# A window-attention kernel: 26 fewer pairs of always-met waits ahead of the causal attention, and each layer's weights requested in eight parts

## The reference: what is computed

```
x = layernorm(x + causal_attention(x))      # 16 heads of 8, rotary, full causal softmax
x = layernorm(x + window_layers(x))         # 6 layers, see below
x = layernorm(x + memory(x))                # circular convolution and a decayed sum over time
x = layernorm(x + routed_experts(x))        # 8 experts, top 2, limited capacity
```

```
x = attn_layer(shift_tokens(x), Wqkv[i], q_scale[i], k_scale[i], Wo[i]) + x
x = ffn_layer(shift_tokens(x), ln_g[i], ln_b[i], W1[i], b1[i], W2[i], b2[i]) + x
```

## Time and profile before

| | |
|---|---|
| median of three runs | 2211.4 us (2200.99, 2211.4, 2215.6) |
| profiled execution | 2203.34 us, its span 2201.5 us |
| mean granted TensorE clock | 0.939 of full speed |
| PE / DVE / ACT / POOL busy | 88% / 79% / 68% / 58% of the span |
| causal attention | from the start to about 412 us |
| window layers | about 415 to 2000 us |
| memory and experts | the rest |

### The profile page before, as it was taken

One profiled execution on the slowest core, in us unless ns is written; L12 is line 12 of the kernel. 1 busy time (PEld: TensorE's weight loads), 2 busy tenths in 40 slices (PEclk: granted clock), 3 DMA queues, 4 the chain that ended last, 5 costly groups with the idle time before them and its releaser, 6 DMA issues. The chain is left out here.

```text
span 2201.5 us, 68287 instructions
## 1 busy us (share of the span) xinstructions
PE 1941.5 (88%) x26493; PEld 1304.8 (59%) x26493; DVE 1738.5 (79%) x3617; ACT 1502.7 (68%) x2952; POOL 1267.1 (58%) x1132
## 2 busy tenths in 40 slices
PE   5788898589999999999999999999999999984283
PEld 2333333246777777777677776777677777762162
DVE  4666654578999999999899998999999999844623
ACT  2256556457888788878787877888788878854123
POOL 4500000278777877787677777777777787711053
PEclk8699989889999999999999999999999999996587
DMA  6312100201111121111211113111311111101612
GB/s 159 110 43 45 23 3 2 70 28 41 31 41 31 40 69 52 32 41 31 81 41 40 32 31 91 31 41 31 91 31 41 31 41 31 41 21 27 195 37 69
DMA packets 70612, 108.18 MB, mean 49 GB/s; under 512 B 20887, under 2 KB 47774, under 8 KB 68734
## 3 DMA queue, kind: packets, MB, share of 16 engines
q1 hardware_dynamic: 68262, 100.87, 16.0%
q0 software_dynamic: 1280, 2.62, 0.4%
q10 hardware_dynamic: 752, 0.33, 0.1%
HBM read 41.60 MB, written 12.26 MB: 24 GB/s over the span
## 5 line engine op out<-in xcount | busy, mean ns | idle before, releaser
L1730 POOL TENSOR_TENSOR qk<-rot_cos,rot_sin 128x512 f32<-128x512 f32 x256 | 324.2, 1274 | 95.9 <-DVE rot_sin L1476 95.3
L1740 POOL TENSOR_TENSOR qk<-qk,rnorm 128x512 f32<-128x512 f32 x256 | 263.1, 1044 | 139.4 <-DVE rnorm L1509 139.4
L1474 DVE TENSOR_TENSOR rot_cos<-pA,layer_tab 128x512 f32<-128x512 f32 x384 | 264.0, 688 | 55.7 <-ACT sq L1258 42.0
L437 ACT ACTIVATE probs_by_key<-pT 128x512 f32<-128x512 f32 (+3 forms) x384 | 177.3, 489 | 159.3 <-PE pT L320 124.5
L1486 DVE TENSOR_REDUCE sumsq<-sq 128x8 f32<-128x512 f32 x384 | 257.6, 672 | 30.5 <-ACT sq L1258 30.4
L502 DVE TENSOR_REDUCE minus_max<-pS 128x1 f32<-128x1024 f32 (+7 forms) x256 | 184.7, 754 | 117.7 <-PE pS L290 117.0
L1476 DVE TENSOR_TENSOR rot_sin<-pA,layer_tab 128x512 f32<-128x512 f32 x384 | 261.5, 681 | 0.0
L1258 ACT ACTIVATE sq<-pA 128x512 f32<-128x512 f32 x384 | 231.4, 602 | 29.3 <-PE pA L880 22.7
L1316 ACT ACTIVATE probsT<-pD 64x512 f32<-64x512 f32 x384 | 226.4, 590 | 6.7 <-PE pD L925 4.5
L880 PE MATMUL pA<-W_ahead,x_feature_major 128*128 128x512 f32 x384 | 202.6, 611 | 17.1 <-DVE rot_sin L1476 10.8
L941 PE MATMUL pD<-probsT,v 128*64 128x64 f32 x3072 | 196.4, 223 | 18.0 <-issue 16.6
(11 more groups left out here) (318 smaller groups left out, 4576.4 us busy)
## 6 DMA issues: line engine op xcount, KB each, us to landing
v_shifted<-v SPq DMA_DIRECT2D x96, 384.0 KB, 3.5
v_shifted<-v SPq DMA_DIRECT2D x95, 128.0 KB, 3.4
q_stack<-stacked SPq DMA_DIRECT2D x24, 192.0 KB
k_stack<-stacked SPq DMA_DIRECT2D x24, 192.0 KB
W_ahead<-in_Wqkv_dram SPq DMA_DIRECT2D x12, 384.0 KB
layer_weights<-in_Wqkv_dram SPq DMA_DIRECT2D x12, 384.0 KB
stacked<-part SPq DMA_DIRECT2D x32, 128.0 KB, 2.4
tokens_in<-tokens SPq DMA_DIRECT2D x2, 1024.0 KB
```

What stands on the lines that cost most here:

```text
L437: act.activation(PTr[n % RING][:, 0:q1 - q0], ST[n % 2][:, 0:q1 - q0], AF.Exp, scale=float(AD) ** -0.5).then_inc(exp_done, 1)
L1474: dve.tensor_tensor(t1[c % 2][:, :].rearrange("p (h g d) -> p h g d", g=2, d=32), a, tabl[s % 2][:, j].unsqueeze(1).broadcast_to([P, 8, 2, ...
L1730: pool.tensor_tensor(qk(s, c), t1[c % 2][:, :], t2[c % 2][:, :], ALU.add).then_inc(added[c], 1)
L1740: pool.tensor_tensor(v, v, rn[p % 2][:, o:o + 8].unsqueeze(2).broadcast_to([P, 8, DH]), ALU.mult).then_inc(scaled[c], 1)
```

## The change

It has two parts. FILL goes from 63 to 37 rounds of two waits. And `load_layer` takes a list of parts, of which there are eight: the four chunks of Wqkv (0 to 3), the scales (4), Wo (5), W1 with b1 (6), and W2 with ln_g, ln_b and b2 (7). For the layers that are requested ahead, 2 to 5, SP now issues part k in the step of tile 7 + k of the layer before, ahead of that step's shift, instead of all in the step of tile 8; the wait on x2_done moves to tile 7. Layers 0 and 1 are still requested whole. b1 moves ahead of W2 in the order. The readers' waits are as they were.

```diff
-FILL = 63
+FILL = 37
...
-def load_layer(sp, w, W, l, done):
+def load_layer(sp, w, W, l, done, parts=range(8)):
 
     for c in range(4):
-        sp.dma_start(W[:, c * 768:(c + 1) * 768], w["Wqkv"][l, :, c * 768:(c + 1) * 768]).then_inc(done, 16)
-    for j, (src, h) in enumerate((("q_scale", 0), ("q_scale", 1), ("k_scale", 0), ("k_scale", 1))):
...
+        if c in parts:
+            sp.dma_start(W[:, c * 768:(c + 1) * 768], w["Wqkv"][l, :, c * 768:(c + 1) * 768]).then_inc(done, 16)
+    if 4 in parts:
+        for j, (src, h) in enumerate((("q_scale", 0), ("q_scale", 1), ("k_scale", 0), ("k_scale", 1))):
...
+    if 5 in parts:
+        sp.dma_start(W[:, WO_AT:W1_AT].rearrange("p (g n) -> p g n", n=D),
+                     w["Wo"][l].rearrange("(g p) n -> p g n", p=P)).then_inc(done, 16)
+    if 6 in parts:
+        sp.dma_start(W[:, W1_AT:W2_AT], w["W1"][l]).then_inc(done, 16)
+        for k in range(2):
+            for f, n in FF_CHUNKS:
+                s = B1_AT + 3 * k + f
+                sp.dma_start(W[0:n, s:s + 1], w["b1"][l, k * FF + f * P:k * FF + f * P + n].rearrange("(p a) -> p a", a=1))\
+                    .then_inc(done, 16)
+    if 7 in parts:
+        sp.dma_start(W[:, W2_AT:W2_AT + 2 * D].rearrange("p (g n) -> p g n", n=D),
+                     w["W2"][l, 0:2 * P, :].rearrange("(g p) n -> p g n", p=P)).then_inc(done, 16)
+        sp.dma_start(W[0:FF - 2 * P, W2_AT + 2 * D:W2_AT + 3 * D], w["W2"][l, 2 * P:FF, :]).then_inc(done, 16)
+        for k, src in enumerate(("ln_g", "ln_b", "b2")):
+            sp.dma_start(W[:, LN_AT + k:LN_AT + k + 1], w[src][l, :].rearrange("(p a) -> p a", a=1)).then_inc(done, 16)
+
+
+PARTS_AT = [(0,), (1,), (2,), (3,), (4,), (5,), (6,), (7,), ()]
...
             for s in range(STEPS):
-                if s % TILES == 8 and s > TILES:
-                    sp.wait_ge(x2_done, s // TILES * PB)
-                    load_layer(sp, w, W[(s // TILES + 1) % 2], s // TILES + 1, w_loaded[(s // TILES + 1) % 2]) if s // TILES + 1 < DEPTH else None
+                ahead = s // TILES + 1
+                if s % TILES >= 7 and s > TILES and ahead < DEPTH:
+                    if s % TILES == 7:
+                        sp.wait_ge(x2_done, s // TILES * PB)
+                    load_layer(sp, w, W[ahead % 2], ahead, w_loaded[ahead % 2], PARTS_AT[s % TILES - 7])
```

More of the change, by code:

```diff
@@ new lines, in load_layer @@
+        if c in parts:
+            sp.dma_start(W[:, c * 768:(c + 1) * 768], w["Wqkv"][l, :, c * 768:(c + 1) * 768]).then_inc(done, 16)
+    if 4 in parts:
+        for j, (src, h) in enumerate((("q_scale", 0), ("q_scale", 1), ("k_scale", 0), ("k_scale", 1))):
+            s = SC_AT + j * DH
+            if h == 0:
+                sp.dma_start(W[:, s:s + DH], w[src][l:l + 1, :].broadcast_to([P, DH])).then_inc(done, 16)
+            else:
+                sp.dma_start(W[:, s:s + 32], w[src][l:l + 1, 32:64].broadcast_to([P, 32])).then_inc(done, 16)
+                sp.dma_start(W[:, s + 32:s + 64], w[src][l:l + 1, 0:32].broadcast_to([P, 32])).then_inc(done, 16)
```

## The result

| | changed | before |
|---|---|---|
| median of 19 runs each | 2198.99 us (2187.25 to 2209.94) | 2211.87 us (2200.99 to 2233.78) |
| ratio, 95% interval | 0.9935 (0.991 to 0.996) | |
| profiled execution, its span | 2190.26 us, 2188.4 us | 2203.34 us, 2201.5 us |
| mean granted clock | 0.939 | 0.939 |

The change makes the kernel faster by 0.65%, inside the 1% that I called no change. I had forecast 24 us more; it is 13 us less, and outside my range.

A forecast was written before the change was run, and what follows sets the result against it. The prediction took PE, running a hand-written order, to bound the kernel. Layer-change cost 34.8, less 10.8 for the spread and 0 for the waits, gave +24.0 us on a mean of 2207.8: 2232 us, range 2212 to 2256.

The forecast's parts named there:

- the 1% that I called no change: Whole kernel: about 1%, 22 us, cannot be told from no change; chances slower 0.58, within 1% 0.37, faster 0.05.
- the one on the waits: PE's queue before the first key stack: 52 wait instructions fewer, costed at 0, with 0 to 4.1 us gained.
- the first score matmul: Sign in the causal stage: PE's first score matmul still at 42 to 43 us, ended by the DMA.
- The pause at the layer change: Four changes into layers 2 to 5: PE waits 6.4 us for the last part; with slow clock 8.7 each, 34.8 in all.
- 2.4 us later against 2.2: Layer change: b2, the last transfer of the last part, lands 2.2 us after its issue ends, at 913.7.
- The pair's excess less the pause: Layer-change pairs: PE's slow clock behind the pause costs 2.3 us each.
- The burst's gaps: Window-layer pairs issuing 23 weight transfers: spreading them removes 7.60 us of gaps and two slow stretches, gaining 10.8 us.
- My reading: PE's "issue" gaps in the four burst pairs, 7.60 us in all: instruction fetch held up behind the burst, inferred.
- The rule that I weighed: Skill text: code streams in 16 KiB blocks, hidden; so "issue" gaps are not fetch and may stay: +34.8, 2243, chance 0.15.
- The favourable one: Rival: the causal stage's slow stretches go away, with the waits at most 36.7 us gained, 2195 in full; chance 0.10.
- the slow stretch of 310 to 340 us: Causal stage: clock 0.60 on average, 140 matmuls against 213 in the 30 us before, priced at 10.3 us.
- its other place: Causal stage, 65 to 105 us: 124 matmuls at clock 0.50, 280 in the next 40 us, priced at most 22.3 us.

The follow-up runs named there:

- e1: The kernel before with only FILL changed from 63 to 37, weights still in one burst: 2161.18 us, ratio 0.9799.
- the seven kernels named above: The kernels with a gap in nearly every round between 560 and 1900 us: the kernel before, e2, e4, e6, e7, e9 and e12.
- e6: e3 with FILL changed from 37 to 60: 2181.79 us, ratio 0.9834.
- e2: The changed kernel with FILL put back from 37 to 63, so only the eight parts remain: 2236.89 us, ratio 1.012.
- e5: e3 with FILL at 63 and 230 pairs of met waits at the head of PE's window-layer list: 2180.72 us, ratio 0.9851.
- e11: e3 with FILL changed from 37 to 15: 2164.76 us, ratio 0.9799.
- e4: The changed kernel with the 26 removed pairs of waits put at the head of PE's window-layer list: 2251.44 us, ratio 1.0172.
- e9: e3 without the met waits that the helper `spare` writes, so a round is 1014 instructions instead of 1024: 2241.17 us, ratio 1.0108.
- e12: e3 with FILL changed from 37 to 0, no met waits ahead of the causal stage: 2236.39 us, ratio 1.0141.
- e7: e3 with 64 pairs of met waits at the head of PE's window-layer list, FILL 37: 2266.07 us, ratio 1.0223.
- e3: The changed kernel with parts 0 and 1 together at tile 7 and every later part one tile earlier: 2160.93 us, ratio 0.9791.

## Why the prediction was wrong, step by step

**The step that failed** is the one on the waits. I costed FILL at 0 to 4.1 us gained and wrote that it "also shifts PE's program against its fetch blocks and the clock's steps; I give that no sign". That shift is the change's largest term: e1 changes nothing else and is 2% faster than before. I had the clue in hand, "issue" gaps and an instruction queue of 214 packets, and could have counted 1024 instructions a round, 256 a block, and therefore a border on the same matmul of every round. The number of waits was off too, 26 instructions fewer and not 52, since two waits share one. That matters here only because it is the count that moves the border. Of the step's own subject I was right: the first score matmul came at 41.83 for 42.54 us, its idle time 9.92 for 9.93 and ended by the same DMA.

**The pause at the layer change** was right in place, cause and size: 6.6 to 6.8 us against 6.4, in all 36.0 against 34.8. b2 was issued at 893.72 and PE went on at 896.12, 2.4 us later against 2.2. Behind the pause the clock is at 0.50 up to 898 us and back at 1.00 by 900. The pair's excess less the pause is 1.6 to 2.9 us each time, 2.3 forecast.

**The burst's gaps** went, and 11.1 us with them, 10.8 forecast. My reading was half right: code that comes late. In the longest of the four, PE stops at 1078.35 and the packet starts only at 1078.79; it takes 1.15 us, within what others take, and PE goes on 1.27 us after it. The packets of this kernel's other gaps all start while PE is still at work. So there the fetch was late to start. The half that I missed is the border: the matmuls behind the gaps of the earlier trace rows stand at 196 modulo 256 as well. With the borders elsewhere (e1) the same bursts cost 1.0 to 1.4 us a pair, and the 0.61 us gap that is left there stands at a border too.

**The rule that I weighed**, of the same section of the Trainium skill, says that fetching is hidden, since instructions are issued more slowly than blocks arrive. The traces do not bear that out for this kernel: in the seven kernels named above the gaps stand at one position modulo 256, follow it when it is moved, and end 1.2 to 1.7 us behind a packet. Where long matmuls run the traces agree with it: borders there cost nothing that the rows show, but for the one just behind a dense run (e6) and those in the bursts.

**The rivals.** The favourable one put the slow stretch of 310 to 340 us at 10.3 us. It is indeed not there in the changed kernel, 211 matmuls at clock 1.00, and the causal stage is 9.9 us shorter; from 65 to 105 us, its other place, the clock is 0.60 with 143 matmuls for 124. But this does not follow FILL. In e2 and e5 PE's list is that of the kernel before up to the end of the causal stage, and the stretch at half clock is missing (202 and 215 matmuls from 310 to 340 us, clock 0.94 and 1.00). In e11, with FILL at 15, it is back (143 at 0.60). In e4 one of the same length stands at 198.5 us. So the 9.9 us are not shown to be the change's doing. Whether they are a difference between executions stays open, with one profile of each kernel.

**What stays open.** The traces don't show which of PE's instructions a packet carries, nor what passes in the 1.2 to 1.7 us between its end and PE's next matmul. How far ahead PE's instructions are issued is not measured either, and with it why the position inside a run matters as it does: a border behind 83 of the small matmuls costs nearly nothing, one behind 93 to 127 costs 0.9 to 1.9 us (e9, e12), one behind 172 or 178 costs 0.6 to 1.2 (e7), one behind 191 or 192 costs 0.1 to 1.1 (before, e2, e4, e6). In e9 and e12 the first run of a round shows the gap from 93 on, the second only from 125. Nor is it explained why e11 gets by at 94. Last, e1 is 44 us faster than the kernel before by their ratio, and the pairs of the two traces account for 36 of it.

## What to carry to other kernels

An engine's program is data with an alignment. Where a long unrolled loop has a burst of very short instructions, count instructions modulo 256, see that a round is a multiple of 256, and place the border where long instructions run. The sign is a row of "issue" gaps that always stand behind the same number of matmuls, and end just behind a packet of the instruction queue. A part that prefetches should be issued so that its last transfer does not stand behind a step that the waiting engine itself has to finish first: one tile earlier was worth 34 us of trace here, 38 between the medians. With both, at 2161 us, the kernel is 2% faster than before and some 1.5% faster than the change as made (0.9791 / 0.9935).

## What the runs showed that I had not expected

- A wait that is already met is not free on PE and not costless to remove: 0.11 us each at the head of a stage (26 in 2.9 us, 230 in 25.0), and as filler it moves the code: 64 more than e3 has made the kernel 105 us slower (e7), 256 more made it 20 us slower (e5).
- The same four bursts of 23 transfers cost 11.4 us in their pairs at one place of the borders and 4.7 at another.
- A fetch of 16.4 KB of PE's code takes 0.88 to 1.6 us, and PE goes on 1.2 to 1.7 us after it; four of these in every round go unseen unless the short matmuls run out first.
